# Weight preparation moved into the slots of the first sequence's attention, under a newly searched timetable of side work

## The reference

```python
x = x + attn(layernorm(x))       # 16 heads of 16; scores (q k)^2, causal, divided by their sum
x = x + ffn(layernorm(x))        # int8 weights / 127, 768 hidden: down(silu(gate) * up)
x = x + m(layernorm(x))          # m(x) = x + mamba_f(xn) + flip(mamba_b(flip(xn)))
x = x + fp4_ffn(x)               # fp4 quantised inputs, weights, hidden; 704 hidden

def mamba(x):                    # inner width 512, 16 states
    u, z = split(x @ Win.T)
    u = silu(conv4(u) + convb)                    # causal, four taps, one channel each
    dtr, B, C = split(u @ Wx.T)
    dt = softplus(dtr @ Wdt.T + bdt)
    h[t] = exp(dt[t] * -exp(Alog)) * h[t-1] + dt[t] * u[t] * B[t]
    y[t] = h[t] @ C[t] + D * u[t]
    return (y * silu(z)) @ Wout.T
```

## Time and profile before

| | us |
|---|---|
| median of 3 runs (lowest, highest) | 6630.95 (6627.23, 6632.68) |
| profiled execution | 6625.01 |
| its span in the profile | 6623.3 |
| granted TensorE clock, share of full speed | 0.84 |
| start to the first scan | 281.1 |

### The profile page before, as it was taken

How to read it: one execution, slowest core, us unless ns; L and a number is a source line. 1 busy time by engine, 2 the same in 40 slices (tenths; PEclk the granted TensorE clock), 3 DMA queues, 4 the chain that set the end, 5 groups by cost and what they waited for, 6 DMA issues and landing times. The chain is left out here.

```text
span 6623.3 us, 79907 instructions
## 1 busy us (share of the span) xinstructions
PE 4595.8 (69%) x21853; PEld 2953.3 (45%) x21900; DVE 4712.6 (71%) x6052; ACT 4210.5 (64%) x7080; POOL 4672.7 (71%) x2442
## 2 busy tenths in 40 slices
PE   5666677676777777676776777777677776767565
PEld 3344354443544444354443544444354444544443
DVE  4467686777768677686777768677686777768774
ACT  3476666667666666666667666666666667666562
POOL 0377767777777777767777876777777777776784
PEclk7787888888888888898888888888898888888777
DMA  3111111111111111111111111111111111111110
GB/s 114 37 36 47 42 52 41 52 46 34 58 40 47 43 54 50 39 50 42 51 46 34 60 38 47 46 50 51 39 50 43 52 44 40 54 39 42 43 44 27
DMA packets 152786, 308.71 MB, mean 47 GB/s; under 512 B 20870, under 2 KB 58310, under 8 KB 149926
## 3 DMA queue, kind: packets, MB, share of 16 engines
q1 hardware_dynamic: 152278, 302.80, 14.4%
HBM read 285.90 MB, written 16.84 MB: 46 GB/s over the span
## 5 line engine op out<-in xcount | busy, mean ns | idle before, releaser
L762 POOL TENSOR_TENSOR arena_m<-bS,arena_m 128x1024 f32<-128x1024 f32 x1024 | 2413.3, 2367 | 454.5 <-DMA bS<-brow 248.1
L1267 DVE TENSOR_TENSOR_SCAN arena_m<-psum,arena_m 128x512 f32<-128x512 f32 x2048 | 2437.4, 1209 | 161.1 <-ACT psum L990 125.3
L1564 PE MATMUL psum<-ident,arena_m 128*128 128x128 f32 x8192 | 1466.2, 316 | 1177.2 <-ACT hc L998 965.0
L1564 PEld LDWEIGHTS psum<-ident,arena_m 128*128 128x128 f32 x8192 | 1096.9, 162 | 1820.6 <-issue 1020.9
L990 ACT ACTIVATE psum<-arena_m,Aneg 128x512 f32<-128x512 f32 x2048 | 1414.6, 697 | 718.2 <-DVE arena_m L1267 695.3
L773 POOL TENSOR_TENSOR arena_m<-arena_m,hc 128x1024 f32<-128x1024 f32 x512 | 1212.8, 2369 | 460.2 <-ACT hc L998 354.7
L1278 DVE SCALAR_TENSOR_TENSOR arena_m<-psum,Ct,arena_m 128x512 f32<-128x512 f32 x1024 | 754.0, 737 | 681.3 <-PE psum L1564 679.0
L998 ACT ACTIVATE hc<-psum,Ct 128x512 f32<-128x512 f32 x1024 | 696.4, 680 | 38.9 <-PE psum L1564 38.6
L859 ACT ACTIVATE arena_a<-psum 128x512 f32<-128x512 f32 (+3 forms) x1024 | 380.3, 441 | 465.3 <-PE psum L1377 303.9
L1377 PE MATMUL psum<-arena_a 64*128 64x512 f32 (+3 forms) x2048 | 467.2, 562 | 160.0 <-ACT arena_a L859 56.4
L708 POOL TENSOR_SCALAR_AFFINE_SELECT arena_a<-arena_a 128x512 f32<-128x512 f32 x256 | 159.2, 637 | 540.5 <-ACT arena_a L859 540.5
(11 more groups left out here) (140 smaller groups left out, 7113.6 us busy)
## 6 DMA issues: line engine op xcount, KB each, us to landing
bS<-brow SPq DMA_DIRECT2D x512, 256.0 KB, 3.3
wB<-kept_B SPq DMA_DIRECT2D x16, 1408.0 KB, 6.2
wU<-kept_U SPq DMA_DIRECT2D x32, 512.0 KB, 5.6
wO<-kept_O SPq DMA_DIRECT2D x32, 512.0 KB, 5.7
wU<-kept_Z SPq DMA_DIRECT2D x32, 512.0 KB, 5.4
wA<-kept_A SPq DMA_DIRECT2D x16, 768.0 KB, 5.7
wB<-kept_B SPq DMA_DIRECT2D x16, 768.0 KB, 5.8
wA<-kept_A SPq DMA_DIRECT2D x16, 640.0 KB, 3.9
```

Source lines behind the costliest of these rows:

```text
L762: pool.tensor_tensor(hb[s % HBS][:, two, :], bS[:, s % 2, :].unsqueeze(1).to_broadcast([P, 2, T]), du[r][:, two, :], ALU.mult).then_inc(m_ ...
L1267: dve.tensor_tensor_scan(v, EB[j % EBS], v, 0.0, ALU.mult, ALU.add).then_inc(m_scan.sem, 1)
L1564: ins = pe.transpose(HT[i % 2][:, m * P:(m + 1) * P], hb[s % HBS][:, m, i * P:(i + 1) * P], ident[:, :])
```

## The change

1. SP issues the norm vectors `ng` and `nb` first, then the first sequence's input and attention weights (slots 96 and 116 of sequence -2), and all other weights behind them, at the end of sequence -2 (`load_weights`). ScalarE waits at its start for the two vectors only.
2. The 26 turn jobs that stood ahead of the first slot go into slots 6 to 16 (int8) and 28 to 42 (Mamba) of sequence -1, the fp4 jobs into 44 to 51 and 57 to 59, each evicted one slot later. The casts stand at DVE's slots 4 to 6, the 54 fp4 operations one by one in slots 10 to 52, the decay rates at slot 45. Three buffers move (`wA` and `hc` take staged weights), and the jobs use five PSUM banks in turn.
3. The stores are three: int8 at slot 0, Mamba at 40, fp4 at 66. SP waits at slot 0 until the int8 jobs are done.
4. The table of slots is replaced throughout. Rows of one piece hold the same parts on the same engines; their slots differ. `a_v` and `a_q` on PE get waits that only `a_k` had, since their order may now differ.

```diff
+        INT8_OUT, MAMBA_OUT, FP4_OUT, KEPT, FREE = 0, 40, 66, 77, 92
+        CASTS = (4, 5, 6)
+        JOB_SLOT = list(range(6, 6 + NJ8)) + list(range(28, 28 + NJ - NJ8)) + [44, 45, 46, 47, 48, 49, 50, 51] + [57, 57, 58, 58, 59, 59]
+        FP4_SLOT = [10 + q * 43 // (6 * QOPS) for q in range(6 * QOPS)]
+        DECAYS = 45
...
+            def store_int8():
+
+                sp.wait_ge(setup_act.sem, NJ8 // 2)
+                sp.wait_ge(setup_dve.sem, (NJ8 + 1) // 2)
+                sp.dma_start(kept["A0"], d_gu0_flat).then_inc(stored8.sem, 16)
+                sp.dma_start(kept["B0"].rearrange("p (k n) -> p k n", k=NF), d_dn0).then_inc(stored8.sem, 16)
+                sp.wait_ge(stored8.sem, 16 * STORES8)
...
             def one(b):
                 for j in range(SLOTS):
-                    if first(b) and FP4_DVE <= j < FP4_DVE + 6:
-                        fp4_weights(j - FP4_DVE)
-                    n = NJ + j - FP4_PE - 1
-                    if first(b) and NJ <= n < NJ4 and n % 2 == 0:
-                        evict(n)
+                    if first(b) and j in CASTS:
+                        cast(CASTS.index(j))
+                    for n in turned_in(b, j - 1):
+                        if n % 2 == 0:
+                            evict(n)
+                    for q in range(6 * QOPS):
+                        if first(b) and FP4_SLOT[q] == j:
+                            fp4_weights(q)
...
-            for n in range(NJ):
-                turn_weights(n)
             pe.wait_ge(const_set.sem, 5 + G)
-            pe.wait_ge(setup_act.sem, NJ // 2)
-            pe.wait_ge(setup_dve.sem, (NJ + 1) // 2)
...
-        row("a_mask", None, 1, POOL=[11, 12, 18, 18, 23, 26, 29, 29, 31, 36, 37, 37, 42, 44.1, 46, 46])
+        row("a_mask", None, 1, POOL=[14, 17, 17, 19, 21, 25, 26, 26, 29, 32, 36, 37, 41, 45, 46, 46])
...
-        row("p_rows", 1, 0, SP=[26])
+        row("p_rows", 1, 0, SP=[45])
```

More of the change, by code:

```diff
@@ L205, in block_kernel @@
         SB = [psum[:, EBS + 2 + i, :] for i in range(3)]
-        loaded = {k: signal(f"loaded_{k}") for k in ("ffn", "mamba", "small", "fp4")}
+        loaded = {k: signal(f"loaded_{k}") for k in ("small", "vectors", "cast0", "cast1", "cast2", "mamba0", "mamba1", "fp40", "fp41", "fp42")}
         ones_set = signal("ones_set")
@@ L424, in first, with second @@
             return isinstance(b, int) and b == -1
+        def second(b):
+            return isinstance(b, int) and b == -2
         def take_bank(pe, b, piece, r, n):
@@ L680, in one @@
                     side("SP", work, b, j)
+                    if second(b) and j == SLOTS - 1:
+                        load_weights()
                     sb_, jb = spot(b, j + 7)
@@ L1073, in evict, with fp4_weights @@
                 dve.tensor_copy(dst, src).then_inc(setup_dve.sem, 1)
-            for n in range(0, NJ, 2):
-                evict(n)
-            def fp4_weights(part):
+            def fp4_weights(q):
+                part, k = divmod(q, QOPS)
                 s, c = divmod(part, 2)
@@ L1082, in fp4_weights @@
                 half = cols // 2
-                dve.wait_ge(loaded["fp4"].sem, 16 * 3)
-                if part:
-                    dve.wait_ge(wquant.sem, QOPS * part)
-                for k in range(QOPS):
-                    quantise(s_fp4[s][0:rows, c * half:(c + 1) * half], wtmp[0:rows, 0:half], w_am, w_sc, w_inv, 0, wquant,
-                             QOPS * part, k)
+                if k == 0:
+                    dve.wait_ge(loaded[f"fp4{s}"].sem, 16)
+                    if part:
+                        dve.wait_ge(wquant.sem, QOPS * part)
+                quantise(s_fp4[s][0:rows, c * half:(c + 1) * half], wtmp[0:rows, 0:half], w_am, w_sc, w_inv, 0, wquant,
+                         QOPS * part, k)
             def norm_stat(n, b, src, k):
@@ L1568, in one @@
                 for j in range(SLOTS):
-                    if first(b) and 0 <= j - FP4_PE < NJ4 - NJ:
-                        turn_weights(NJ + j - FP4_PE)
+                    for n in turned_in(b, j):
+                        turn_weights(n)
                     tb, jt = spot(b, j - TURN)
```

296 lines of the change are left out of this document (154 added, 142 removed).

## The result

| | before | after |
|---|---|---|
| median of 4 runs (lowest, highest), us | 6631.3 (6627.2, 6632.7) | 6430.0 (6421.1, 6433.2) |
| profiled execution, us | 6625.0 | 6432.1 |
| span in the profile, us | 6623.3 | 6430.3 |

The account below looks back on a forecast made before the run. No engine is full, so waits set the time. From the profiled 6625.0, first part -51 and loop -75 gave 6499; with the median 6 above, 6505 us, range 6430 to 6595.

Parts of the forecast that it names:

- the term for the table's other moves: Loop: new positions of masks, softplus sums and the like, costed at zero, bounds -4 to +5 us a period.
- The term for SP's slots: Loop: no B-row load behind an unmet wait; a third of POOL's 14.3 us counts, -5 a period, bounds 0 and 10.
- First part: Start to first scan: inputs first, stall gone, interleave cost; -51 us (-60 to -32), first scan near 230.
- Inputs first: Start of the run: input loaded before most weights, statistics near 7 us instead of 35.2; -28 us (-30 to -24).
- The stall of 28: First score stage: PE's 27.79 us wait behind DVE's fp4 block goes when the block is spread; -28 us.
- the interleave: First score stage: casts, turns and fp4 work spread beside attention make divisions wait; +5 us (0 to +20).
- Loop: Fifteen periods at -5 us each, all from SP's slots; -75 us, bounds -10 and +2 a period.
- each engine's sum of work per sequence is the same: Loop: the timetable removes and adds no work; only positions move.
- rival C: Loop: POOL waits before masks 6 to 9, moved ahead of ScalarE's squares; +7 a period, 6685 us; chance 0.08.
- The tail: After the last scans: the last FFN alone, 114.7 us, a chain no table shortens; 0.
- Rival B: Loop: waits off B-row loads wholly on the path, table gains 9 us a period or more; 6445 us; chance 0.17.
- The signs named beforehand: Right: first scan near 230, PE idle under 10, POOL's B-row wait under 3, period 389 to 394; wrong: after 250, 395 up.

Follow-up runs that it names:

- `old_table`: Changed preparation of weights and inputs loaded first, with every row of the slot table as in the kernel before; 6570.8 us, ratio 0.9918.
- `old_sp`: Changed kernel with SP's old slots (loads, two saves, store), and one DVE division ahead of two statistics steps at slot 24; 6466.4 us, ratio 0.9763.
- `norm_pool3_v`: Changed kernel with three norms' short steps on POOL, and the second half of `a_v` at slots 123 and 124 instead of 125.2 and 127; 6336.3 us.
- `new_back`: Changed preparation, SP's new slots; other engines' new slots only for side work that stood at slot 52 and later, the rest old; 6557.1 us, ratio 0.9888.
- `new_front`: Changed preparation, SP's new slots; other engines' new slots only for side work from old slots 0 to 51; DVE division reordered at slot 24; 6512.6 us.
- `new_sp_only`: Changed preparation and the old slot table, but with SP's new slots (loads, two saves, store); 6618.9 us, ratio 0.9991 to the kernel before.
- `old_norm_pool`: Changed preparation and the old slot table, SP's old slots too, with all five norms' short steps on POOL; 6553.8 us, ratio 0.9895.

## Why the prediction missed

**The step that failed** is the term for the table's other moves: "I cost at zero with a spread", -4 to +5 us a period. `old_table` and `old_sp` differ in these moves, and they take the period from 396.0 to 386.9, 9 us. The term for SP's slots, -5 a period, then measured half a microsecond (386.9 to 386.4). So the loop's gain lay where the forecast had put nothing, and the term that it had argued for is nearly absent from the period.

**First part: -51 forecast, -41 measured.** The forecast's terms describe the preparation, and for it they hold: 281.1 to 230.6 is -50.5. Inputs first was -28, and the start of the statistics moved by 29.5 in `old_table`. The stall of 28 went, and the interleave cost 27.8 less (95.5 - 70.3), that is 2.6, where I took 5. Some 4 us were lost before the first score and behind the last division, where I had no term. (The lower bound of -60 doesn't come from its terms, which give -58.) The error lies in another term that wasn't in the sum: the new table's effect on the first part, costed at nothing, is +9.3: 1.1 before the first score, 6.1 in the score stage, 2.1 behind it. Undoing the late value projection gives back 10.3 in `norm_pool3_v`, enough for the whole. But it isn't the projection alone: `new_back`, which has it too, starts its scans at 236.4 with a score stage of 70.8, and `new_front`, with the old projection and the new scores, at 232.9 with a stage of 76.1. How the 9.3 divide among the rows stays open.

**Loop: -75 forecast, -147 measured from first to last scan.** By medians the other moves without SP's rows bring 6571 - 6466 = 105 us, beyond the bound of -4 a period. (It is less than 15 times 9, as in `old_sp` the first scan comes 10.5 later and the first period takes 9.5 more than in `old_table`.) SP's rows give +48 us in the old table and -36 in the new, where -75 was forecast. SP's step itself went as told (saves behind their bS, POOL's wait for bS gone), and "a third of it counts" is near what it brings when the norms' steps are off DVE (2 to 3 us a period in the old table). It missed in the kernel as it is by the premise "each engine's sum of work per sequence is the same". DVE's busy time depends on what POOL does beside it. I had the row for this, used it only for the first part, and put the like of it in the loop at zero. This premise hid a cost and no gain: without three of the blocked norms the changed kernel would have been 101 us faster still. It can't explain why the kernel beat the forecast.

**What the other moves do.** In the changed kernel 59 us are the convolution's rows, -35 (a loss) is `q_norm` at slot 50, nothing is the masks, of which rival C had made a danger: POOL's wait before masks fell from 134.9 to 119.3. From `old_table` to `old_sp` the gain shows in slots 16 to 23 (33.9 to 25.4 us), 32 to 39 (26.8 to 22.3) and 112 to 119 (32.9 to 29.4), and slots 48 to 55 lose 3.4. The old convolution's rows bring back only 3.2 us of the first. What is left sits in rows not taken apart: 81 us if the moves are worth 105, as without SP's rows, and 165 if they are worth 189, as with them. Its cause stays open. Late loads cost nothing, as forecast: PE waits for no DMA in the changed kernel. The tail, forecast at 0, was 4.9 us shorter; with only one of the two parts of the table it is 114.1 (`old_sp`) or 115.0 (`new_sp_only`), and I did not look into why.

**Luck, and the rivals.** Errors of both signs stood in the sum: too much for SP, nothing for the other moves, nothing for the table's 9.3 in the first part. That the total came so near the range is luck. The terms' own bounds, -10 for the waits and -4 for the rest, would have allowed -14 a period, and the forecast's -10 left the second out. Rival B had the time nearest (6445), and this was luck too. `new_sp_only` refutes its reason, and its price of 9 didn't follow from its condition: all of the waits on the path would be 14.3.

**The signs named beforehand.** Period under 389 and first scan at 239.9, not 230, both pointed away from the forecast's sum, in opposite directions. No idle of PE over 10 us in the score stage, and no wait of POOL for bS, came as told, and the second of these said nothing about the time.

## What to carry to other kernels

A wait that goes may have been the gap in which another engine's blocked instruction ran: before a wait is priced, look at what the engines beside it do in that time, and compare the durations of one instruction form over its occurrences, not only the idle times. Equal instruction counts with more busy time are the sign for it in the page. In this kernel chains of short steps with two SBUF inputs on DVE did not belong beside a POOL that ran without gaps; they were better where POOL waited anyway, or on POOL, but not in a stretch that POOL bounds. And when every row of a timetable moves, an unchanged sum of work is no reason for a term of zero: here the moves so costed were worth 9 us a period.

## What the runs showed of the hardware

- A DVE step on 128x4 numbers takes about 0.16 us, and in the changed kernel up to 2.32 beside a POOL instruction on 128x1024. The step with one input, `ve<-mv` (L1131), was stretched too, from 0.17 to 1.51. A blocked step ends with POOL's instruction and not its own 0.16 behind it (2698.30 and 2698.29; 2700.60 and 2700.59); in the earlier trace rows too the addition took 0.35 more than its like, while the mask beside it had 0.50 left to run. A chain of four can be blocked at three of its steps, as POOL's next instruction starts in the 0.04 us between two steps. The scans, with one input in PSUM, were not stretched: 1.16 to 1.23 us in 2048 cases.
- On POOL the same steps take 0.19 to 0.22 us each on average, hardly more than on DVE undisturbed. (In `old_norm_pool` single ones took up to 0.86.)
- While the weights load, an issue on SP can take 11.14 us (the load of `Wx` at 10.07 of the changed kernel), where others take 0.45.
